# A mixture-of-experts layer on one core: the low passes of four row tiles in the second matmul are formed from seven half products

## What is computed

```python
buf = jnp.zeros((E, B, capacity, C), dtype=x.dtype)
buf = buf.at[e_flat, b_idx, pos_c].add(x_rep * keep[..., None].astype(x.dtype))
h = jax.nn.relu(jnp.einsum('ebnc,ech->ebnh', buf, W1) + b1[:, None, None, :])
y = jnp.einsum('ebnh,ehc->ebnc', h, W2) + b2[:, None, None, :]
y_tok = y[e_flat, b_idx, pos_c]
...
x = x + gb * _L0_ffn_ref(h, ...)
```

## Time and profile before

| | |
|---|---|
| device time, 3 runs | 2168.45, 2169.28, 2170.48 us; median 2169.28 |
| span of the profiled execution, first to last instruction | 2170.2 us |
| TensorE (PE) busy | 2138.0 us |
| VectorE (DVE) busy | 1640.0 us |
| ScalarE (ACT) busy | 1042.6 us |
| GpSimd (POOL) busy | 379.1 us |
| mean granted clock of TensorE | 0.998 of full speed |

### The profile page before, as it was taken

How to read it: one execution, slowest core, us unless ns; L and a number is a source line. 1 busy time by engine, 2 the same in 40 slices (tenths; PEclk the granted TensorE clock), 3 DMA queues, 4 the chain that set the end, 5 groups by cost and what they waited for, 6 DMA issues and landing times.

```text
span 2170.2 us, 33701 instructions
## 1 busy us (share of the span) xinstructions
PE 2138.0 (99%) x12526; PEld 1181.9 (54%) x12526; DVE 1640.0 (76%) x2901; ACT 1042.6 (48%) x2050; POOL 379.1 (17%) x335
## 2 busy tenths in 40 slices
...
GB/s 288 246 266 234 242 253 142 185 181 122 167 190 167 156 129 150 79 102 127 132 107 112 142 88 117 112 146 78 110 134 112 98 127 153 76 102 98 44 6 25
DMA packets 353205, 300.94 MB, mean 139 GB/s; under 512 B 242475, under 2 KB 242731, under 8 KB 352528
## 3 DMA queue, kind: packets, MB, share of 16 engines
...
q0 software_dynamic: 21904, 42.14, 10.4%
...
## 4 chain that ended last, share of the span: by engine, by line
PE 92%; DVE 3%; issue 1%; DMA 1%; SPq 1%; ACT 0%; POOL 0%; another core or an unknown queue 0%; DVEq 0%; ACTq 0%; POOLq 0%
PE bank L2078 37%; PE bank L2004 32%; PE bank L1920 20%; PE bank L1869 1%; DMA reg_e<-reg_e 1%; PE bank L1992 1%; PE bank L2057 0%; DVE reg_c L1698 0%; SPq L502 0%; DVE wmx L1425 0%; DVE reg_e L1279 0%; DVE reg_b L1481 0%; PE bank L1880 0%; DVE reg_e L1150 0%; PE bank L1882 0%
## 5 line engine op out<-in xcount | busy, mean ns | idle before, releaser
L2078 PE MATMUL bank<-reg_b,reg_c 128*128 128x512 f16 x3792 | 824.0, 379 | 0.9 <-DVE reg_b L1481 0.9
L2078 PEld LDWEIGHTS bank<-reg_b,reg_c 128*128 128x128 f16 x3792 | 370.5, 98 | 444.4 <-issue 2.3
L1920 PE MATMUL bank<-reg_c 128*128 128x512 f16 x2296 | 505.4, 379 | 1.8 <-ACT reg_e L887 1.2
L2004 PE MATMUL bank<-reg_e,reg_a 128*128 128x320 f16 x2880 | 447.5, 299 | 0.0
L1920 PEld LDWEIGHTS bank<-reg_c 128*128 128x128 f16 x2296 | 222.0, 98 | 259.4 <-ACT reg_e L887 1.7
L2004 PEld LDWEIGHTS bank<-reg_e,reg_a 128*128 128x128 f16 x2880 | 280.9, 98 | 112.7
L768 POOL DMA_INDIRECT out_dram<-reg_e,midx x79 | 142.4, 1802 | 1002.7 <-DVE reg_e L1529 881.9
L980 ACT ACTIVATE reg_e<-bank,b1s 128x320 f32<-128x320 f32 x120 | 63.3, 527 | 407.6 <-PE bank L2004 407.5
L2004 PE MATMUL bank<-reg_e,reg_d 128*128 128x320 f16 x1440 | 232.5, 299 | 0.0
L1525 DVE SCALAR_TENSOR_TENSOR reg_e<-bank,inv,reg_e 128x512 f32<-128x512 f32 x79 | 59.1, 748 | 225.7 <-PE bank L2078 225.7
L2004 PEld LDWEIGHTS bank<-reg_e,reg_d 128*128 128x128 f16 x1440 | 139.7, 98 | 57.6 <-ACT reg_e L980 4.0
...
## 6 DMA issues: line engine op xcount, KB each, us to landing
...
```

What stands on the lines that cost most here:

```text
L1920: ins = mm(dst[:, :], wqs[:, ws, kc, e0:e0 + P], xns[:, j % 2, xs, kc, :], start=kc == 0 and xs == 0 and ws == 0, stop=kc == KC - 1 and ws ...
L2004: ins = mm(dst[:, 0:CAP], w[ws][:, c, p * P:(p + 1) * P], xs_of[:, KC * xs + 2 * i + c, j * CAP:(j + 1) * CAP], start=first and c == 0 and ...
L2078: ins = mm(bank_y[i % 2][:, :], hid[:, hs, hc, t * P:(t + 1) * P], w2s[:, ws, hc, :], start=k == 0 and hs == 0 and ws == 0, stop=k == HC - ...
```

## The change

In u = 0 of experts 1 to 7 (`shared(v)`, seven units) the second layer is `second_layer_shared`. Four row tiles are taken as two groups g = 0, 1 of two tiles (0 and 1, 3 and 4). The low passes of a group (high x low and low x high; 4 blocks: two tiles by two halves of the hidden width, times two halves of W2) are formed from seven half products of 16 matmuls of 128x256 in place of eight, from sums of `hid` and of `w2s` that VectorE makes in float16 (`hid_sum`, `w2_sum`). Parts that go to more than one block are copied on ScalarE (`copy_p1`, `copy_p6`, `copy_p7`) and added into PSUM on VectorE (`add_12`, `add_22`). The high passes are then accumulated on top, 16 matmuls of 128x512 for each tile (`high_pass`). Tile 2 keeps its 48 matmuls (`rest_chunks`), cut in three. The order of the tiles is now 2, 0, 1, 3, 4, and the five results lie in five banks, three of which the next unit's first products use.

The sums lie in `stage_q`'s place, so the fill with the next expert's W1 for its maximum waits for the last half product; four of its eight pieces, `scale_head` and `scale_tail` move from this second layer into the following unit's pairs.

```diff
@@ SP @@
-                        if e + 1 < E:
-                            bring_w1(e + 1, fill_max(e + 1, 0), 0)
                         next_unit(2 * e + 1)
                     if e + 1 < E:
+                        if e > 0:
+                            sp.wait_ge(s_prod, prod(e, 4, 1))
+                            bring_w1(e + 1, fill_max(e + 1, 0), 0)
@@ ACT @@
+            def copy_p6(e, g):
+                wait(act, s_prod, prod(e, 6, g))
...
+                a.activation(copy_1[:, g, :], low[g][:, 0:HALF], ACT.Copy).then_inc(s_copy, 1)
@@ DVE @@
+            def w2_sum(e, k):
...
+                if k == 2:
+                    wait(dve, s_tsum, sum_t(e, 1))
+                    wait(dve, s_prod, prod(e, 5, 1))
+                    ins = v_.tensor_tensor(t_sum[:, :, :, :], w2_part(1, 1), t_sum[:, :, :, :], ALU.subtract)
...
+            def hid_sum(e, k, g):
...
+                if k == 2:
+                    wait(dve, s_ssum2, sum_s(e, 1, g))
+                    wait(dve, s_prod, prod(e, 5, g))
+                    ins = v_.tensor_tensor(dst, dst, hid_part(g, 0, 0), ALU.subtract)
...
+                    if u == 1 and e + 1 < E:
+                        if e and t in W1_MAX:
+                            max_piece(e + 1, 0, 4 + W1_MAX.index(t))
@@ PE @@
                 if k == SLOT_P2:
                     wait(pe, s_c11, n)
+                    if p == 0 and shared(v - 1):
+                        wait(pe, s_yd, UT * v)
                     product(bank_p2, w_12, x_raw, 1, 0, p, True, True).then_inc(s_p2, 1)
...
                 if k == SLOT_P5:
                     wait(pe, s_c12, n - 1)
+                    if p == 0 and shared(v - 1):
+                        wait(pe, s_yd, UT * v + 2)
...
+            def low_passes(dst, a_part, b_part, first):
+                for k in range(NP):
+                    for hs, ws in ((1, 0), (0, 1)):
+                        ins = mm(dst, a_part[:, hs, k, :], b_part[:, ws, k, :], start=first and k == 0 and hs == 1,
+                                 stop=False, skip_group_check=True)
+                return ins
...
+            def second_layer_shared(v):
+                e, n = v // 2, pairs_to(v + 1)
+                left, right = slice(0, HALF), slice(HALF, D)
+                rest_chunks(v, 0, NP)
+                for g in range(2):
+                    low_passes(low[g][:, left], hid_part(g, 0, 0), w2_part(0, 0), True)
+                    wait(pe, s_ssum2, sum_s(e, 1, g))
+                    wait(pe, s_tsum, sum_t(e, 1))
+                    low_passes(low[g][:, right], s_sum[:, g, :, :, :], t_sum, False).then_inc(s_prod, 1)
+                for g in range(2):
+                    wait(pe, s_copy, copied(e, 0, g))
+                    low_passes(top[g][:, left], hid_part(g, 0, 1), w2_part(1, 0), False)
+                rest_chunks(v, NP, 3 * HC // 4)
+                for g in range(2):
+                    wait(pe, s_ssum2, sum_s(e, 2, g))
+                    wait(pe, s_tsum, sum_t(e, 2))
+                    low_passes(low[g][:, left], s_sum[:, g, :, :, :], t_sum, False).then_inc(s_prod, 1)
+                for g in range(2):
+                    wait(pe, s_padd, padd(e, 1, g))
+                    wait(pe, s_ssum2, sum_s(e, 3, g))
+                    wait(pe, s_tsum, sum_t(e, 3))
+                    low_passes(low[g][:, left], s_sum3[:, g, :, :, :], t_sum3, False).then_inc(s_prod, 1)
+                for g in range(2):
+                    wait(pe, s_ssum2, sum_s(e, 4, g))
+                    low_passes(top[g][:, right], s_sum[:, g, :, :, :], w2_part(1, 1), False)
+                for g in range(2):
+                    wait(pe, s_padd, padd(e, 2, g))
+                    wait(pe, s_tsum, sum_t(e, 4))
+                    low_passes(low[g][:, left], hid_part(g, 1, 1), t_sum, False).then_inc(s_prod, 1)
+                rest_chunks(v, 3 * HC // 4, HC).then_inc(s_mm2, 1)
+                for g in range(2):
+                    for r, dst in enumerate((top[g], low[g])):
+                        high_pass(dst, (0, 1, 3, 4)[2 * g + r]).then_inc(s_mm2, 1)
```

More of the change, by code:

```diff
@@ L257, in build_program, with shared, tiles, out_bank @@
         bank_u, bank_p2, bank_v = bank[0:3], bank[6], [bank[3], bank[5]]
+        top, low = [bank[4], bank[7]], [bank[6], bank[3]]
+        def shared(v):
+            return v >= SHARED and v % 2 == 0
+        def tiles(v):
+            return SHARED_TILES if shared(v) else tuple(range(UT))
+        def out_bank(e, u, i):
+            if shared(2 * e + u):
+                return (bank_u[pairs_to(2 * e + 1) % 3], top[0], low[0], top[1], low[1])[i]
+            return bank_y[i % 2]
+        def hid_part(g, r, c):
+            t = (0, 1, 3, 4)[2 * g + r]
+            return hid[:, :, c * NP:(c + 1) * NP, t * P:(t + 1) * P]
+        def w2_part(r, c):
+            return w2s[:, :, r * NP:(r + 1) * NP, c * HALF:(c + 1) * HALF]
+        def sum_s(e, k, g):
+            return 8 * (e - 1) + SUM_S[k, g]
+        def sum_t(e, k):
+            return 4 * (e - 1) + SUM_T[k]
+        def prod(e, k, g):
+            return 8 * (e - 1) + 2 * PRODUCTS.index(k) + g + 1
+        def copied(e, k, g):
+            return 6 * (e - 1) + 2 * k + g + 1
+        def padd(e, k, g):
+            return 4 * (e - 1) + 2 * (k - 1) + g + 1
         s_const = sem("s_const")
@@ L1520, in outputs @@
                 wait(dve, s_gate, 7 * e + 3 * u + 3)
-                if u == 0 and t == 0:
+                if u == 0 and i0 == 0:
                     wait(dve, s_inv, e + 1)
@@ new lines, in add_12, with add_22, beside_shared @@
+            def add_12(e, g):
+                wait(dve, s_copy, copied(e, 1, g))
+                v_.tensor_tensor(top[g][:, HALF:D], low[g][:, HALF:D], copy_1[:, g, :], ALU.add).then_inc(s_padd, 1)
+            def add_22(e, g):
+                wait(dve, s_copy, copied(e, 2, g))
+                v_.tensor_tensor(low[g][:, HALF:D], low[g][:, HALF:D], copy_2[:, g, :], ALU.add).then_inc(s_padd, 1)
+            def beside_shared(e, i0):
+                more = e + 1 < E
+                if i0 == 0:
+                    hid_sum(e, 1, 1)
+                    w2_sum(e, 3)
+                    hid_sum(e, 3, 0)
+                    hid_sum(e, 3, 1)
+                    hid_sum(e, 2, 0)
+                    w2_sum(e, 2)
+                    hid_sum(e, 2, 1)
+                    add_12(e, 0)
+                    hid_sum(e, 4, 0)
+                    add_12(e, 1)
+                    hid_sum(e, 4, 1)
+                    w2_sum(e, 4)
+                    add_22(e, 0)
+                    add_22(e, 1)
+                    x_sums(2 * e + 1)
+                if i0 == 1:
+                    x_lo(2 * e + 1)
+                if i0 in (2, 3) and more:
+                    for k in range(2 * i0 - 4, 2 * i0 - 2):
+                        max_piece(e + 1, 0, k)
```

152 lines of the change are left out of this document (121 added, 31 removed).

## The result

| | before | changed |
|---|---|---|
| device time, median (4 runs each, in turn) | 2169.13 us (2168.45 to 2170.48) | 2220.31 us (2218.4 to 2220.59) |
| ratio to before, 95% interval | | 1.0232 (1.022 to 1.0244) |
| span of the profiled execution | 2170.2 us | 2218.8 us |
| mean granted clock of TensorE | 0.998 | 0.989 |

The account below looks back on a forecast made before the run. TensorE's gapless stream was taken to bound the kernel. Gain -22.1, output waits 6 x 7.2 + 4.1 and late fills 3.6 made +28.8 us: 2170.2 became 2199.0, given as 2198 us on the median's scale, range 2166 to 2240.

Parts of the forecast that it names:

- The gain on TensorE: Changed second layer: fewer 512-column, more 256-column matmuls save 3.15 us a unit, 22.1 us for seven if nothing waits.
- The sums on VectorE: Float16 sums in the changed second layer take 2.3 and 1.2 us, so TensorE does not wait for them.
- the rival of long sums: Sums take 4.4 and 2.3 us, delaying TensorE 10.6 us more a unit: 2272 us; chance 0.10.
- The outputs' chain: VectorE waits for scatters before `yo`, delaying next unit's P2': 7.2 us in six units, 4.1 in expert 7.
- The prediction's clock: Timetable of one changed unit, T = 0 at its first second-layer matmul; TensorE wants P2' at 54.4, C11 ends 61.6.
- The rival of busy queues: Each output scatter takes 7.6 to 8.5 us, 11 to 13 us a unit: 2227 to 2244 us; chance 0.10.
- the two rivals in which it hides: Scatter waits not binding, 2157 us, or 2147 without waits (chance 0.12); waits equal to the gain, 22 us (0.06).
- The fill behind the slot-2 maximum: Next unit's pairs: W2 fill for slot 9's maximum, startable only after slot 2's, 0.6 us late six times, 3.6 us.

Follow-up runs that it names:

- the kernel where nothing waits: Changed kernel with four `yo` buffers, one weight maximum before output 4, others in slots 5, 9, 19, W2's first in slot 13: 2147.46 us.
- Four buffers against two: Changed kernel with four `yo` buffers in place of two, output i waiting for scatter i-4 instead of i-2: 2153.56 us, against 2220.31 us.
- the kernel before with nothing but a wait in it: Kernel before, with TensorE waiting before P5 of second units for two, three or six unneeded ScalarE copies: 2189.96, 2210.17, 2240.52 us.
- the kernel with three buffers: Changed kernel with three `yo` buffers in place of two: 2185.63 us, ratio 1.0065.
- The kernel with two buffers and the other slots: Changed kernel, two `yo` buffers kept, one maximum before output 4, others in slots 5, 9, 19, W2's first in slot 13: 2210.64 us.
- the maxima between the outputs' instructions (2194.9): Changed kernel, two `yo` buffers kept, four late weight maxima moved from pair slots to between the two instructions of outputs 3 and 4: 2194.85 us.

## Why the prediction was right in direction and 22 us short

**The gain on TensorE: right.** 0.109 us for a matmul of 256 columns and 3.15 us a unit, forecast from the 96 at the kernel's end; 22.1 us forecast, 22.2 measured in the kernel where nothing waits.

**The sums on VectorE: right, the short ones.** The groups of two of them by line and form, with the adds (count, busy us and mean ns, idle before and what ended it):

```profile
L1832 DVE TENSOR_TENSOR reg_d<-reg_c 128x2048 f16<-128x2048 f16 x14 | 17.2, 1226 | 2.3 <-DVE reg_c L1710 1.4
...
L1807 DVE TENSOR_TENSOR reg_d<-reg_b 128x4096 f16<-128x4096 f16 x7 | 16.0, 2284 | 0.0
...
L1849 DVE TENSOR_TENSOR bank<-bank,reg_e 128x256 f32<-128x256 f32 x14 | 6.1, 433 | 28.6 <-ACT reg_e L1127 28.6
```

2284 and 1226 ns, where the lower bounds were 2.3 and 1.2 us: the rival of long sums falls, and with it its 2272 us. The Trainium skill's 1224 ns for 2048 elements (VectorE: DVE Perf Modes, the perf-mode tier table), given there for bfloat16, agrees with the 1226 measured for float16. VectorE waits for ScalarE's copies before the adds (28.6 us), and TensorE never waits inside the changed second layer, up to 1888.14.

**The outputs' chain: right, and nearly in its size.** The prediction's clock beside expert 6's:

| T + us | forecast | measured |
|---|---|---|
| first result | 35.7 | 35.6 |
| scatter 0 starts | 38.1 | 38.7 |
| `yo` 2 | 45.8 | 44.7 |
| `yo` 3 | 52.7 | 53.6 |
| result 4 evicted | 54.2 | 55.0 |
| `yo` 4 | 58.6 | 59.2 |
| C11 ends | 61.6 | 62.0 |

TensorE takes P2' at 62.1, 7.7 us behind the nominal 54.4, where 7.2 was the term; expert 7, without maxima, loses 4.9 in all (term 4.1). From start to start scatter 0 took 7.6 to 7.9 us in six units and 6.7 in expert 6; I had 7.7. The lengthened instruction that this came from is there: 3.35 us in the six and 2.61 in expert 6, and expert 7 has its 7.6 us without any fills. Scatter 1 took 8.4 to 8.9 us in the six units with fills, where I had 6.9; scatter 2 was quiet, 5.6 to 5.7, where I had 5.9.

That the sum came so near is in part luck. Scatter 1 took some 1.7 us more than forecast. The last link took 1.0 less: from the start of scatter 2 to `yo` 4 it was 4.9 us (1906.85 to 1911.74) and not 5.9, since the landing releases VectorE, while GpSimd starts its next scatter 0.9 us later and I had priced the link from start to start. The rival of busy queues priced all three scatters at 7.6 to 8.5, and only the second was so. Its own sum was wrong too: +58 to +75 needs 11 to 13 us in all seven units, but expert 7 has no fills. With six such units, 4.1 for expert 7 and 3.6 for the fill it would be +52 to +64, from 2221 us on, so the measured 2220.3 does not tell the two apart; the rows of the scatters do. Four buffers against two, at 66.8 us, show that this chain holds the time; the two rivals in which it hides failed, and they describe instead the kernels with four buffers (2147 us was given as the time with no wait at all; 2147.5 was measured).

**The fill behind the slot-2 maximum: the step that failed.** The term was 0.6 us a unit, from a landing of 3.6 to 4 us against 4 us of products between the two slots (by these figures alone nothing would be late; the 0.6 does not follow from them). What happened in place of both is in VectorE's rows above: the slot-2 maximum ends at 1914.14, the fill takes until 1919.46, and VectorE, itself late, goes through what stands between the slots in less than 2 us. It waited 3.42 us here and 23.6 us over the run:

```profile
DVE wm L1651 <- DMA reg_d<-in_w: 23.6, 8, 4.1
```

The fills of 1880 to 1930 us (line L643) also landed more slowly than those of the earlier trace rows:

```profile
DMA to landing us min/median/max: 3.7/5.6/7.6
```

How much reaches TensorE can be read by unit. The nominal time from the changed unit's start to the next second layer is 97.55 - 3.15 = 94.40 us. The six units of experts 1 to 6 take 105.51 to 106.23, so they lose 11.1 to 11.8, 11.4 on the average. P2' starts in them at T + 61.9 to 62.2, 7.65 late on the average; the other 3.7 come behind P2'. So, in us:

| term of the loss | forecast | by the traces | difference |
|---|---|---|---|
| outputs' chain, six units | 6 x 7.2 | 6 x 7.65 | +2.7 |
| the same, expert 7 | 4.1 | 4.9 | +0.8 |
| behind P2', the fill, six units | 6 x 0.6 | 6 x 3.74 | +18.8 |
| sum | 50.9 | 73.2 | +22.3 |

The gain of 22.1 taken off, that is +51.1, as measured, where +28.8 was forecast. The mistake was to take the slack from the undisturbed timetable: a late VectorE has a backlog and takes the slots as fast as it can, so there is nothing to hide a transfer between two of them.

**The clock after a wait: missing in the prediction, and hidden behind the fill.** The sum priced a wait at its length. Windows after the waits show a granted clock of 0.60 and 0.64, so for much of these stretches TensorE ran at the lower of its two levels (1.2 and 2.4 GHz); it had been idle for 3.17 and 2.66 us before them. The Trainium skill (TensorE: Matmul & The Clock Gate, Part 1) has the array's clock fall when it is idle; the trace agrees, and so does the kernel before with nothing but a wait in it.

I had first put the miss down to this, since 22.2 us of slower matmuls are about what is missing. The chain shown above speaks against it: from 1891.24 to 1922.08 it holds no TensorE at all. The slow products before P2' lie beside the scatters, those behind it beside the fill, and the account of waits and slower matmuls only says in which way TensorE passed a time that others set.

Units of the same program show it too. In expert 4 of the changed kernel (T = 0 at 1445.36) the matmuls between P5 and P2' ran at full speed:

```profile
1500.44 0.98 PE L2171 MATMUL bank<-reg_e,reg_d 128*128 128x320 f16 x6 [3.08 <-DVE reg_e L1612]
1501.25 1.79 PE L2171 MATMUL bank<-reg_e,reg_a 128*128 128x320 f16 x12
1507.37 1.78 PE L2171 MATMUL bank<-reg_e,reg_a 128*128 128x320 f16 x6 [4.33 <-DVE reg_e L1683]
```

The window over them (columns as above) has a granted clock of 1.00:

```profile
1500.30:1504.00 3.70, 2.61 (x18) 1.69 (x18) 0.00 (x0) 0.00 (x0) 0.86 (x1) 1.00 0.57 71
```

Yet P2' came no earlier, at T + 62.0: what the matmuls saved, TensorE waited (4.33 us where expert 6 has 2.66). Expert 2 is the same, with 4.27 us and T + 61.9. For the stretch behind P2' the kernel with three buffers shows it. In its experts 1, 4 and 6 only 0.3 us went into slower matmuls there, and still it took 43.1 to 43.4 us from P2' to the next second layer, where the kernel in which nothing waits takes 39.9 and the changed kernel, with 1.7 to 2.7 us of slower matmuls, 43.4 to 44.0. So the fill alone costs over 3 us. In experts 2, 3 and 5 of that kernel the slow matmuls came after the wait for the fill, nothing covered them, and the stretch took 44.2 to 45.0 us.

The kernel with two buffers and the other slots shows what is beneath. There the fill is in time, and behind P2' the units still lose 1.5 us on the average (8.7 to 10.0 in all, of which 8.0 up to P2'), with no wait in it: slow matmuls alone (1.4 to 1.8 us in five of the six units, 0.1 in one). So taking the fill away brought 2.3 us a unit, not 3.7, which is why 2194 to 2202 us was missed; a later P2' took another part. In a kernel where nothing lies beside it the clock's price is paid in full, as in the three with a bare wait, up to 2.7 us for each on the average.

**What stays open.** Why the second scatter takes some 8.5 us: weight fills run beside it in every such case (259 GB/s while expert 6's was under way, 1897.96 to 1905.97), and expert 7, which has none (40 GB/s), has 6.9, which is still above the 5.6 of a quiet one; no run changed the fills alone. Why a bare wait is followed by more slow matmuls in one unit than in another, and a wait of 8.0 us, on the average, by no more than one of 3.5, is not settled. It touches single figures: expert 7's unit, without fills and maxima in all three kernels, loses 4.9 us in the changed kernel and 6.3 in the two others with two buffers, all of the difference in slow matmuls behind P2'. That the maxima between the outputs' instructions (2194.9) do better with two buffers than the other slots (2210.6), by 16 us, is taken apart as far as this: P2' comes at T + 60.6 on the average there against 62.4, and scatter 2 takes 5.7 us against 7.4, which is 1.7 of these 1.8; the matmuls behind P2' lose 0.7 against 1.5, because two of the six units have slow ones there and not five. Why scatter 2 is longer with the other slots was not tested.
